# Two low halves and one copy of a graph network's flush put in another order, an earlier start of one product, and the first adjacency tile scaled by VectorE

## The chip, the cores and the metric

The kernel runs on one core of a Trainium2 chip. The metric is the time of one execution in microseconds (us) as the device reports it. Of the engines, TensorE is called PE, VectorE DVE, ScalarE ACT and GpSimd POOL in the profile; SP is the engine whose queue issues nearly all transfers (DMAs).

## What is computed

For each of 8 batches there are x (1024 rows of 512) and adj (1024 x 1024). Cut to what matters:

```python
# stage 0: four Gaussian kernels k over the entries of adj
w  = exp(-0.5 * (adj[..., None] - mu[k])**2 / (1e-14 + prec[k]**2))
ws = (w / w.sum(over k)).sum(over the row)            # one weight for each row and kernel
x1 = layernorm(x + concat_k(ws[k] * (x @ W[k].T)))
# stage 1: one of four experts for each batch
top1    = argmax(x1.mean(rows) @ router_w + router_b)
out     = adj @ (x1 @ expert_w[top1])
y       = batchnorm_by_expert(out) * gamma + beta     # sums over all batches of the expert
result  = layernorm(x1 + relu(y))
```

The batch norm needs sums over all batches, so the last stage (bn, relu, addition, layer norm) can start only when `out` is complete for the eighth batch.

## The kernel before, in words

**Tiles.** A batch is cut into T = 8 tiles of 128 rows, 64 tiles in all (TILES). Products of float32 values are made of three float16 products: each operand is cut into a high and a low half. `out` is kept turned, as (x1.T adj.T) through the expert: per batch there are eight z units (four 128-column pieces k of x1 by two halves of 512 rows; 24 matmuls of 128x512 each, into one of the two banks of `ps_z`) and eight o units (12 matmuls each, into the bank `ps_o`, which read the expert's planes `w_sel` and `zT`).

**Loop.** Every engine runs the same loop over n, and each has its work of step n written out by hand. Step n handles the weights of adj tile n, the x1 row block n - 1, the z unit n - 9 (`Z_LAG`) and the o unit n - 13 (`O_LAG`). After tile 63 the loop runs on to empty the pipe. In it `z_unit` and `o_units` say which units belong to which step. `FLUSH` is step 65: in step 64 PE makes z unit 55 (the seventh batch's last) and o unit 51, in step 65 o units 52 to 55 and z unit 56, in steps 66 to 68 z units 57 to 59, in step 69 z 60 and o 56, in step 70 o 57 and z 61, in step 71 o 58 and z 62, in step 72 o 59 and z 63, and after that o 60 to 63. `z_ahead_of_o` (line 289) says in which steps PE puts the z unit first.

**What a z unit waits for and who waits for it.** When PE has finished z unit u, ACT writes the high half (`take_z`, line 668 does the copy), and DVE the low half (`low_z`, line 884) from the same bank. z unit u + 2 needs that low half done, as it writes the same bank, and the first o unit of a half of a batch (`o_product`, k == 0) needs the low half of the fourth z unit of that half: o 52 waits for z 55, o 60 for z 63.

**What an o unit waits for.** ACT copies each o unit out of its bank (`take_o`, line 685) and DVE takes bn_stats of it (`o_stats`, line 904). There is one bank for o units, so o unit u waits until unit u - 1 is copied. From unit 53 on odd units use a second bank, half of `ps_t` (`second_bank`, line 267), which is free once the row sums of the last adj tile are done. The wait is line 1133 of the kernel: with `u > KEPT + 3` (KEPT is 50) only units from 54 on wait for the copy of u - 2 instead.

**DVE in a step** (lines 955 to 993): `y_stats` of x1 block n - 2, `low_z` of the z unit of step n - 1, `y_mean_var` of block n - 2, `o_stats` of the o units of step n - 1, `row_sums` of tile n - 1 (three products with accumulated sums, line 915), and then the additions to x1 (`weighted`, line 937) of block n - 1, mixed with the sums over kernels of tile n (line 953). When the o units of a batch are complete, `o_stats` aggregates four chunks (line 909). POOL cuts adj and x into halves (`cut_adj`, lines 500, 503, 505; `cut_x`) and, for each pair of blocks, normalises x1 and cuts it (`norm_pair`, lines 523 to 542); z units of a batch read these cuts.

**Start.** POOL scales adj tile 0 by 1024 in place (line 500, semaphore `pool_as`), then cuts it. ACT's first Gaussian (line 641) waits for that scaling and for two constants that POOL computes just ahead of it (`pool_gauss`), loads a register, and starts.

**Tail.** After o unit 63 DVE aggregates the last statistics, computes the batch norm's scales with ACT's help, and then the last stage runs over 64 row blocks: PE turns `out` back, DVE adds it to x1 (lines 1058, 1061) and takes statistics, ACT applies scales and squares, POOL normalises, SP stores. x1 and the outputs of the earlier batches were spilled to HBM and come back there. SP's queue is one sequence: the loads that need the space of `x1p` and `adjT` wait for z unit 63, the next ones for o unit 63, and the others and the stores for row blocks of the last stage.

Of the kernel before, what the change touches and what calls it, by code (L numbers as in the profile page):

```python
# [38 lines left out]
Z_LAG = 9  # L39
# [9 lines left out]
def gnn_program(nc, x, adj, mean_rel, prec_rel, w0, router_w, router_b, expert_w, gamma, beta, x1_spill,  # L49
# [15 lines left out]
    with ExitStack() as ctx:  # L65
# [3 lines left out]
        def sem(name):  # L69
            return ctx.enter_context(nc.semaphore(name))  # L70
# [76 lines left out]
        act_bn, act_affine, act_ssq, act_out = (sem(f"act_{k}") for k in ("bn", "affine", "ssq", "out"))  # L147
        pool_small, pool_out, pool_affine = (sem(f"pool_{k}") for k in ("small", "out", "affine"))
        act_lnv, act_std = sem("act_lnv"), sem("act_std")
        dve_nmr, dve_out, dve_affine = sem("dve_nmr"), sem("dve_out"), sem("dve_affine")  # L150

        dve_tot, dve_ws, dve_rest, dve_y, dve_stat, dve_mv = (
            sem(f"dve_{k}") for k in ("tot", "ws", "rest", "y", "stat", "mv"))
# [120 lines left out]
        def z_unit(n):  # L274

            if n <= Z_LAG + 2:
                return ((), (0,), (1, 2))[n - Z_LAG] if n >= Z_LAG else ()
            return range(n - Z_LAG, min(TILES, n - Z_LAG + 1))
# [9 lines left out]

        def z_ahead_of_o(n):

            return n == FLUSH - 1 or (n - O_LAG) % T == 0

        def ps_out(u):
            return ps_t[:, 0, :] if second_bank(u) else ps_o[:]
# [198 lines left out]
        def _(pool):  # L493
            g = nc.gpsimd

            def cut_adj(m):

                tile, cut = adj_in[:, m % ADJ_RING, :], adj_cut[:, m % 2]
                pool.wait_ge(adj_landed[m % ADJ_RING], 16 * (m // ADJ_RING + 1))
                g.tensor_scalar(tile, tile, ADJ_SCALE, 1.0, ALU.mult, ALU.mult).then_inc(pool_as, 1)  # L500
                pool.wait_ge(pool_as, m + 1)
                wait(pool, adj_turned[m % 2], 16 * (m // 2))
                g.tensor_scalar(cut[:, 0, :], tile, 1.0, 1.0, ALU.mult, ALU.mult).then_inc(pool_ah, 1)  # L503
                pool.wait_ge(pool_ah, m + 1)
                g.tensor_tensor(cut[:, 1, :], tile, cut[:, 0, :], ALU.subtract).then_inc(pool_al, 1)  # L505
# [125 lines left out]
        def _(act):  # L631
# [54 lines left out]

            for n in range(LAST):
                if n < TILES:
                    act.wait_ge(pool_as, n + 1)
                    wait(act, dve_ws, NK * (n - 1))  # L690
                    if n == 1:
                        act.wait_ge(pe_w0, C)
                    if n == 0:
                        act.wait_ge(pool_gauss, 2)
                    for j, k in enumerate(OTHERS):
                        if n == 0:
                            load_spread(k)
                        square(n, k, wgt[:, n % 2, j, :])
                if 1 <= n <= 2 * E:
                    e, part_ = expert_half(n - 1)  # L700
                    act.wait_ge(experts_landed[e], 16)
                    s.activation(planes(e)[:, 0, part_], expert_in(e)[:, part_], ACT.Copy, scale=W_SCALE).then_inc(act_whi, 1)
                if n - 1 == FLUSH - 1:
                    take_z(n - 1)
                take_o(n - 1)
                if n - 1 != FLUSH - 1:
                    take_z(n - 1)
                if 0 <= n - 1 < TILES:
                    sum_reciprocal(n - 1)
                if n < TILES:  # L710
                    weigh_others(n)
                    act.wait_ge(pool_al, n + 1)
                    if n == 0:
                        load_spread(SOLO)
                    square(n, SOLO, adj_in[:, n % ADJ_RING, :])
                    weigh_solo(n)
                if n == 0:
                    for c in range(C):
                        act.wait_ge(pe_w0, c + 1)
                        s.activation(w0T[:, 0, c, :], w0_banks[c], ACT.Copy, scale=W0_SCALE).then_inc(act_w0, 1)  # L720
# [76 lines left out]
        def _(dve):  # L797
# [3 lines left out]
            v.memset(ones_h[:], 1.0)  # L801
            v.memset(eps_bn, BN_EPS * (Z_SCALE * W_SCALE) ** 2)
            v.memset(eps_out, OUT_EPS)

            def split_w0():

# [91 lines left out]
            def o_stats(u):  # L898
                b, half, k = u // T, u % T // G, u % G
                if u == TILES - 1:  # L900
                    dve.wait_ge(pe_o, u + 1)
                else:
                    dve.wait_ge(act_o, u + 1)
                v.bn_stats(o_stat[:, b % 2, k, half, :], ps_out(u) if u == TILES - 1 else out_unit(u)).then_inc(dve_ostat, 1)
                if half == 1 and k == 3:
                    dve.wait_ge(dve_ostat, u + 1)
                    v.memset(pad, 0.0)
                    for c in range(C):
                        last = v.bn_aggr(o_mv[:, b, c, :], o_stat[:, b % 2, c, :, :].rearrange("p h s -> p (h s)"))
                    last.then_inc(dve_omv, 1)  # L910

            def row_sums(m):
                dve.wait_ge(act_rec, m + 1)
# [41 lines left out]
            for n in range(LAST):  # L955
                if 0 <= n - 2 < TILES:
                    y_stats(n - 2)
                for u in z_unit(n - 1):
                    low_z(u)
                if 0 <= n - 2 < TILES:  # L960
                    y_mean_var(n - 2)
                for u in o_units(n - 1):
# [11 lines left out]
                    v.tensor_tensor(sumT[:], sumT[:], ps_s[:, C:2 * C], ALU.add).then_inc(dve_sumT, 1)  # L974
                if 0 <= n - 1 < TILES:
                    row_sums(n - 1)
                else:
                    for k in range(5):
                        route(n, k)
# [97 lines left out]
        def _(pe):  # L1077
# [47 lines left out]
            def o_product(u):  # L1125
# [4 lines left out]
                    pe.wait_ge(dve_z, u + G)  # L1130
                if second_bank(u):
                    pe.wait_ge(dve_ws, NK * TILES)
                wait(pe, act_o, u - 1 if u > KEPT + 3 else u)
                for c in range(C):
                    for i, (left, right) in enumerate(PRODUCTS):
                        last = te.matmul(ps_out(u), w_sel[:, left, c, k * P:(k + 1) * P], zT[:, right, half, c, :],  # L1136
# [78 lines left out]
```

## Time and profile before

| | us |
|---|---|
| median of 3 runs | 892.62 |
| lowest and highest | 890.96, 893.26 |
| the profiled execution, its own time | 888.44 |
| span in the profile of that execution | 886.7 |

| engine | busy us | share of the span |
|---|---|---|
| PE matmul | 751.8 | 85% |
| DVE | 754.0 | 85% |
| ACT | 766.9 | 86% |
| POOL | 687.5 | 78% |

The span runs from the first instruction to the last landing, and the execution's own time is 1.7 us longer. A row of the timeline is: start and duration in us, engine, line of the kernel, operation, what it writes <- what it reads, shape, count, and in brackets how long the engine had been idle and for whom it waited. In the chain of waits (the chain that ended last, in order of time) a row is start, duration, engine, tile, line, and how many instructions are merged. A row of the windows view is a stretch of time, its length, the busy us (and instructions) of PE, PEld, DVE, ACT and POOL, the TensorE clock granted as a share of full speed, the mean busy share of the 16 DMA engines (it can come out slightly above 1) and GB/s.

### The profile page before, as it was taken

How to read it: one execution, taken by the hardware profiler on the slowest of the kernel's cores; microseconds unless marked ns; L12 is line 12 of the kernel's file. 1: busy time of each engine (PE TensorE's matmuls, PEld its weight loads, DVE VectorE, ACT ScalarE, POOL GpSimd, SP SyncE). 2: the span in 40 equal slices, each digit the busy share in tenths (PEclk: the TensorE clock that was granted, in tenths of full speed). 3: DMA queues.
4: the chain of work that ended last, by engine and by line, in shares of the span. 5: the costliest groups of instructions: out<-in, count | busy, mean ns of one | idle time of the engine just before them, and what ended most of it. 6: DMA issues, size and time to landing. Idle time of an engine off the chain costs nothing.

```text
span 886.7 us, 12501 instructions
## 1 busy us (share of the span) xinstructions
PE 751.8 (85%) x3922; PEld 349.1 (39%) x3922; DVE 754.0 (85%) x1639; ACT 766.9 (86%) x774; POOL 687.5 (78%) x773
## 2 busy tenths in 40 slices
PE   1444469899999999999999999999999989996671
PEld 1111124344444444444444444444444434444440
DVE  1999988899999999999999999999999981226994
ACT  5999998999999999999999999999999941116983
POOL 6699999999988888888888888888888441004794
PEclk9966679999999999999999999999999999998996
DMA  8799886898897779777977797789786636219999
GB/s 229 200 282 257 189 243 166 221 202 206 201 240 192 192 190 240 196 194 190 237 198 191 195 240 196 192 189 242 198 190 161 124 141 263 95 64 396 356 383 366
DMA packets 263925, 191.71 MB, mean 216 GB/s; under 512 B 210098, under 2 KB 210098, under 8 KB 262322
## 3 DMA queue, kind: packets, MB, share of 16 engines
q1 hardware_dynamic: 263714, 190.90, 79.3%
q8 instruction: 31, 0.51, 0.2%
q14 instruction: 36, 0.29, 0.1%
q10 hardware_dynamic: 144, 0.00, 0.0%
HBM read 91.78 MB, written 48.76 MB: 159 GB/s over the span
## 4 chain that ended last, share of the span: by engine, by line
ACT 38%; DVE 27%; POOL 19%; PE 9%; issue 4%; DMA 1%; SPq 0%; POOLq 0%; DVEq 0%; ACTq 0%
DVE ps_t L953 19%; ACT wgt L647 13%; ACT ps_t L656 6%; ACT ps_t L658 6%; ACT adj_in L641 5%; ACT ps_t L652 5%; PE ps_z L1118 5%; POOL adj_cut L505 3%; DVE x_in L937 3%; DVE wgt L915 3%; PE ps_o L1136 2%; POOL adj_in L500 2%; POOL x_turn L516 2%; PE ps_t L1136 2%; POOL adj_cut L503 2%
## 5 line engine op out<-in xcount | busy, mean ns | idle before, releaser
L1118 PE MATMUL ps_z<-adjT,x1p 128*128 128x512 f16 x1536 | 341.7, 379 | 0.5 <-POOL x1p L542 0.5
L953 DVE TENSOR_TENSOR ps_t<-ps_t,wgt 128x1024 f32<-128x1024 f32 x192 | 234.8, 1223 | 28.0 <-ACT ps_t L652 26.9
L1104 PE MATMUL ps_h<-w0T,x_turn 128*128 128x512 f16 x768 | 194.5, 407 | 75.1 <-DVE x_in L937 64.2
L915 DVE SCALAR_TENSOR_TENSOR wgt<-wgt,ps_t 128x1024 f32<-128x1024 f32 x192 | 224.7, 1214 | 15.8 <-ACT ps_t L658 15.8
L1118 PEld LDWEIGHTS ps_z<-adjT,x1p 128*128 128x128 f16 x1536 | 150.0, 98 | 181.3 <-POOL x1p L542 1.0
L641 ACT ACTIVATE wgt<-adj_in,neg_mu 128x1024 f32<-128x1024 f32 x192 | 205.6, 1134 | 8.4 <-POOL adj_in L500 8.2
L647 ACT ACTIVATE wgt<-wgt 128x3072 f32<-128x3072 f32 x64 | 176.5, 2758 | 0.0
L1136 PE MATMUL ps_o<-zT,w_sel 128*128 128x512 f16 x696 | 159.7, 379 | 4.8 <-DVE zT L884 3.5
L1104 PEld LDWEIGHTS ps_h<-w0T,x_turn 128*128 128x128 f16 x768 | 75.0, 103 | 184.4 <-issue 105.1
L505 POOL TENSOR_TENSOR adj_cut<-adj_in,adj_cut 128x1024 f16<-128x1024 f32 x64 | 136.6, 2134 | 5.4
L1136 PEld LDWEIGHTS ps_o<-zT,w_sel 128*128 128x128 f16 x696 | 67.9, 98 | 87.7 <-DVE zT L884 4.5
L937 DVE SCALAR_TENSOR_TENSOR x_in<-ps_h,wsum,x_in 128x128 f32<-128x128 f32 x256 | 82.4, 343 | 8.9 <-PE ps_h L1104 0.2
L884 DVE SCALAR_TENSOR_TENSOR zT<-ps_z,zT 128x512 f16<-128x512 f32 x64 | 43.1, 673 | 52.2 <-ACT zT L668 52.2
L542 POOL TENSOR_TENSOR x1p<-x_in,x1p 128x512 f16<-128x512 f32 x64 | 76.0, 1187 | 5.3
L516 POOL TENSOR_TENSOR x_turn<-x_in,x_turn 128x512 f16<-128x512 f32 x64 | 74.2, 1159 | 5.3
L500 POOL TENSOR_SCALAR adj_in<-adj_in 128x1024 f32<-128x1024 f32 x64 | 69.5, 1086 | 11.2 <-DMA adj_in<-in_adj_dram 5.9
L641 ACT ACTIVATE adj_in<-adj_in,neg_mu 128x1024 f32<-128x1024 f32 x64 | 72.8, 1138 | 0.0
L503 POOL TENSOR_SCALAR adj_cut<-adj_in 128x1024 f16<-128x1024 f32 x64 | 67.6, 1057 | 5.3
L668 ACT ACTIVATE zT<-ps_z 128x512 f16<-128x512 f32 x64 | 37.2, 582 | 39.3 <-PE ps_z L1118 39.3
L656 ACT ACTIVATE ps_t<-ps_t 128x1024 f32<-128x1024 f32 x64 | 64.6, 1009 | 5.9 <-DVE ps_t L953 3.8
L652 ACT ACTIVATE ps_t<-adj_in 128x1024 f32<-128x1024 f32 x64 | 65.8, 1028 | 3.0 <-DVE wgt L915 0.6
L658 ACT ACTIVATE ps_t<-ps_t 128x1024 f32<-128x1024 f32 x64 | 64.5, 1008 | 2.0
(220 smaller groups left out, 774.2 us busy)
## 6 DMA issues: line engine op xcount, KB each, us to landing
adj_in<-in_adj_dram SPq DMA_DIRECT2D x64, 512.0 KB, 4.1
x_in<-in_x_dram SPq DMA_DIRECT2D x64, 256.0 KB, 4.3
x_spill<-x_in SPq DMA_DIRECT2D x28, 512.0 KB, 3.4
out_spill<-o_stage SPq DMA_DIRECT2D x50, 256.0 KB, 3.1
w_sel<-w_planes SPq DMA_DIRECT2D x8, 1024.0 KB, 7.5
adjT<-x_spill SPq DMA_DIRECT2D x6, 1024.0 KB, 10.1
out_dram<-adjT SPq DMA_DIRECT2D x5, 1024.0 KB, 6.7
adjT<-out_spill SPq DMA_DIRECT2D x4, 1024.0 KB, 12.7
```

What stands on the lines that cost most here:

```text
L505: g.tensor_tensor(cut[:, 1, :], tile, cut[:, 0, :], ALU.subtract).then_inc(pool_al, 1)
L641: s.activation(to, adj_in[:, n % ADJ_RING, :], ACT.Square, bias=neg_mu[:, k:k + 1], scale=spread[k]).then_inc(act_sq, 1)
L647: s.activation(w, w, ACT.Exp, scale=-1.0).then_inc(act_w, 1)
L652: s.activation(tot, adj_in[:, n % ADJ_RING, :], ACT.Exp, scale=-1.0).then_inc(act_solo, 1)
L656: s.activation(tot, tot, ACT.Ln, scale=SUM_SCALE).then_inc(act_ln, 1)
L658: s.activation(tot, tot, ACT.Exp, scale=-1.0).then_inc(act_rec, 1)
L915: v.scalar_tensor_tensor(out=wgt[:, m % 2, j, :], in0=wgt[:, m % 2, j, :], scalar=SUM_SCALE / W0_SCALE, in1=tot, op0=ALU.mult, op1=ALU.mul ...
L937: last = v.scalar_tensor_tensor(out=row[:, f], in0=ps_h[:, m % 2, f], scalar=wsum[:, m % 2, COLUMN[k]:COLUMN[k] + 1], in1=row[:, f], op0=A ...
L953: v.tensor_tensor(tot, tot, wgt[:, n % 2, j, :], ALU.add).then_inc(dve_tot, 1)
L1104: last = te.matmul(ps_h[:, n % 2, :], xT[:, n % 2, left, c, :], w0T[:, right, c, :], start=(c + i == 0), stop=(c == C - 1 and i == 2))
L1118: last = te.matmul(ps_z[:, u % 2, :], x1p[:, b % 2, left, t, k * P:(k + 1) * P], adjT[:, b % 2, right, t, half * HALF:(half + 1) * HALF], ...
L1136: last = te.matmul(ps_out(u), w_sel[:, left, c, k * P:(k + 1) * P], zT[:, right, half, c, :], start=(c + i == 0), stop=(c == C - 1 and i = ...
```

## The change

1. **Start.** DVE instead of POOL scales adj tile 0, as soon as the tile has landed (`dve_as`). POOL's cut of the tile and ACT's first Gaussian wait for DVE. POOL's count `pool_as` is one lower for all later tiles.
2. **Seventh batch's last z.** In DVE's step 64 the low half of z unit 55 is made right behind `row_sums(63)`, ahead of the additions to x1 of block 63, and no longer in step 65 behind `y_stats(63)`.
3. **One more unit in the free bank.** o unit 53 waits for the copy of o unit 51 and no longer for that of 52.
4. **Last z.** In step 72 PE makes z unit 63 ahead of o unit 59, and ACT makes the high half of z 63 ahead of the copy of o 59.
5. **Statistics.** For the last batch the aggregation of chunk k follows its own bn_stats, so one aggregation instead of four stands behind the last o unit. Each of the four has a wait and a one-column memset of its own.

```diff
@@ -147,7 +147,7 @@
         act_bn, act_affine, act_ssq, act_out = (sem(f"act_{k}") for k in ("bn", "affine", "ssq", "out"))
         pool_small, pool_out, pool_affine = (sem(f"pool_{k}") for k in ("small", "out", "affine"))
         act_lnv, act_std = sem("act_lnv"), sem("act_std")
-        dve_nmr, dve_out, dve_affine = sem("dve_nmr"), sem("dve_out"), sem("dve_affine")
+        dve_nmr, dve_out, dve_affine, dve_as = sem("dve_nmr"), sem("dve_out"), sem("dve_affine"), sem("dve_as")
 
         dve_tot, dve_ws, dve_rest, dve_y, dve_stat, dve_mv = (
             sem(f"dve_{k}") for k in ("tot", "ws", "rest", "y", "stat", "mv"))
@@ -288,7 +288,11 @@
 
         def z_ahead_of_o(n):
 
-            return n == FLUSH - 1 or (n - O_LAG) % T == 0
+            return z_taken_first(n) or (n - O_LAG) % T == 0
+
+        def z_taken_first(n):
+
+            return n in (FLUSH - 1, TILES - 1 + Z_LAG)
 
         def ps_out(u):
             return ps_t[:, 0, :] if second_bank(u) else ps_o[:]
@@ -497,8 +501,11 @@
 
                 tile, cut = adj_in[:, m % ADJ_RING, :], adj_cut[:, m % 2]
                 pool.wait_ge(adj_landed[m % ADJ_RING], 16 * (m // ADJ_RING + 1))
-                g.tensor_scalar(tile, tile, ADJ_SCALE, 1.0, ALU.mult, ALU.mult).then_inc(pool_as, 1)
-                pool.wait_ge(pool_as, m + 1)
+                if m == 0:
+                    pool.wait_ge(dve_as, 1)
+                else:
+                    g.tensor_scalar(tile, tile, ADJ_SCALE, 1.0, ALU.mult, ALU.mult).then_inc(pool_as, 1)
+                    pool.wait_ge(pool_as, m)
                 wait(pool, adj_turned[m % 2], 16 * (m // 2))
                 g.tensor_scalar(cut[:, 0, :], tile, 1.0, 1.0, ALU.mult, ALU.mult).then_inc(pool_ah, 1)
                 pool.wait_ge(pool_ah, m + 1)
@@ -686,11 +693,12 @@
 
             for n in range(LAST):
                 if n < TILES:
-                    act.wait_ge(pool_as, n + 1)
+                    wait(act, pool_as, n)
                     wait(act, dve_ws, NK * (n - 1))
                     if n == 1:
                         act.wait_ge(pe_w0, C)
                     if n == 0:
+                        act.wait_ge(dve_as, 1)
                         act.wait_ge(pool_gauss, 2)
                     for j, k in enumerate(OTHERS):
                         if n == 0:
@@ -700,10 +708,10 @@
                     e, part_ = expert_half(n - 1)
                     act.wait_ge(experts_landed[e], 16)
                     s.activation(planes(e)[:, 0, part_], expert_in(e)[:, part_], ACT.Copy, scale=W_SCALE).then_inc(act_whi, 1)
-                if n - 1 == FLUSH - 1:
+                if z_taken_first(n - 1):
                     take_z(n - 1)
                 take_o(n - 1)
-                if n - 1 != FLUSH - 1:
+                if not z_taken_first(n - 1):
                     take_z(n - 1)
                 if 0 <= n - 1 < TILES:
                     sum_reciprocal(n - 1)
@@ -801,6 +809,8 @@
             v.memset(ones_h[:], 1.0)
             v.memset(eps_bn, BN_EPS * (Z_SCALE * W_SCALE) ** 2)
             v.memset(eps_out, OUT_EPS)
+            dve.wait_ge(adj_landed[0], 16)
+            v.tensor_scalar(adj_in[:, 0, :], adj_in[:, 0, :], ADJ_SCALE, None, ALU.mult).then_inc(dve_as, 1)
 
             def split_w0():
 
@@ -902,12 +912,16 @@
                 else:
                     dve.wait_ge(act_o, u + 1)
                 v.bn_stats(o_stat[:, b % 2, k, half, :], ps_out(u) if u == TILES - 1 else out_unit(u)).then_inc(dve_ostat, 1)
-                if half == 1 and k == 3:
+                chunks = range(C) if k == 3 else ()
+                if b == NB - 1:
+                    chunks = (k,)
+                if half == 1 and chunks:
                     dve.wait_ge(dve_ostat, u + 1)
                     v.memset(pad, 0.0)
-                    for c in range(C):
+                    for c in chunks:
                         last = v.bn_aggr(o_mv[:, b, c, :], o_stat[:, b % 2, c, :, :].rearrange("p h s -> p (h s)"))
-                    last.then_inc(dve_omv, 1)
+                    if k == 3:
+                        last.then_inc(dve_omv, 1)
 
             def row_sums(m):
                 dve.wait_ge(act_rec, m + 1)
@@ -955,8 +969,9 @@
             for n in range(LAST):
                 if 0 <= n - 2 < TILES:
                     y_stats(n - 2)
-                for u in z_unit(n - 1):
-                    low_z(u)
+                if n != FLUSH:
+                    for u in z_unit(n - 1):
+                        low_z(u)
                 if 0 <= n - 2 < TILES:
                     y_mean_var(n - 2)
                 for u in o_units(n - 1):
@@ -974,6 +989,9 @@
                     v.tensor_tensor(sumT[:], sumT[:], ps_s[:, C:2 * C], ALU.add).then_inc(dve_sumT, 1)
                 if 0 <= n - 1 < TILES:
                     row_sums(n - 1)
+                    if n == FLUSH - 1:
+                        for u in z_unit(n):
+                            low_z(u)
                 else:
                     for k in range(5):
                         route(n, k)
@@ -1130,7 +1148,7 @@
                     pe.wait_ge(dve_z, u + G)
                 if second_bank(u):
                     pe.wait_ge(dve_ws, NK * TILES)
-                wait(pe, act_o, u - 1 if u > KEPT + 3 else u)
+                wait(pe, act_o, u - 1 if u > KEPT + 2 else u)
                 for c in range(C):
                     for i, (left, right) in enumerate(PRODUCTS):
                         last = te.matmul(ps_out(u), w_sel[:, left, c, k * P:(k + 1) * P], zT[:, right, half, c, :],
```

## Rows read from the trace of the kernel before

**Rows 1.** Windows view: one stretch of the loop, one of the last stage

```profile
160.00:720.00 560.00, 546.26 (x2913) 248.69 (x2912) 529.53 (x1095) 550.35 (x507) 485.63 (x529) 1.00 0.80 198
...
812.00:876.00 64.00, 40.50 (x249) 27.80 (x247) 62.90 (x199) 54.78 (x115) 56.12 (x85) 0.93 1.03 379
```

**Rows 2.** ACT's waits, 20 to 721 us: total, times, longest

```profile
ACT ps_t L656 <- DVE ps_t L953: 3.8, 6, 1.0
```

**Rows 3.** The chain of waits, one o unit in the flush

```profile
784.80 2.59 PE ps_t L1136 x12
```

**Rows 4.** PE's waits, 700 to 887 us, for the low halves

```profile
PE ps_o L1136 <- DVE zT L884: 3.5, 2, 2.1
```

**Rows 5.** Timeline, the start

```profile
9.05 1.05 POOL L500 TENSOR_SCALAR adj_in<-adj_in 128x1024 f32<-128x1024 f32 x1
...
10.66 3.23 ACT L641 ACTIVATE wgt<-adj_in,neg_mu 128x1024 f32<-128x1024 f32 x3 [8.23 <-POOL adj_in L500]
...
25.84 1.20 DVE L967 SCALAR_TENSOR_TENSOR x1p<-adjT,x1p 128x1024 f16<-128x1024 f32 x1
...
25.92 2.03 POOL L500 TENSOR_SCALAR adj_in<-adj_in 128x1024 f32<-128x1024 f32 x1
```

**Rows 6.** Issue of adj tile 0 (timeline) and its time to landing (transfers view)

```profile
1.20 0.42 SPq L318 DMA_DIRECT2D adj_in<-in_adj_dram  x1
...
adj_in<-in_adj_dram SPq DMA_DIRECT2D x1, 512.0 KB, 6.8
```

**Rows 7.** Durations (ns, min/median/max) of two DVE lines that scale float32 in SBUF

```profile
L1027 DVE TENSOR_SCALAR wgt<-wgt,b_sb x4: 409/410/414, 808.8 to 809.7; 128x256 f32<-128x256 f32 x4
...
L1073 DVE TENSOR_SCALAR adjT<-adjT,adj_in x2: 535/726/916, 874.4 to 874.9; 128x512 f32<-128x512 f32 x2
```

**Rows 8.** Timeline, the flush of the seventh batch

```profile
725.18 1.13 DVE L937 SCALAR_TENSOR_TENSOR x_in<-ps_h,wsum,x_in 128x128 f32<-128x128 f32 x4
...
725.61 0.60 ACT L685 ACTIVATE adj_cut<-ps_o 128x512 f32<-128x512 f32 x1 [1.99 <-PE ps_o L1136]
...
726.95 0.67 DVE L884 SCALAR_TENSOR_TENSOR zT<-ps_z,zT 128x512 f16<-128x512 f32 x1
...
727.68 2.76 PE L1136 MATMUL ps_o<-zT,w_sel 128*128 128x512 f16 x12 [2.11 <-DVE zT L884]
...
730.48 0.60 ACT L685 ACTIVATE wgt<-ps_o 128x512 f32<-128x512 f32 x1 [4.27 <-PE ps_o L1136]
...
731.22 2.75 PE L1136 MATMUL ps_t<-zT,w_sel 128*128 128x512 f16 x12 [0.78 <-ACT wgt L685]
...
733.39 1.16 POOL L542 TENSOR_TENSOR x1p<-x_in,x1p 128x512 f16<-128x512 f32 x1
...
738.99 5.34 PE L1118 MATMUL ps_z<-adjT,x1p 128*128 128x512 f16 x24
```

**Rows 9.** Timeline, the last z unit and the last statistics

```profile
787.23 5.34 PE L1118 MATMUL ps_z<-adjT,x1p 128*128 128x512 f16 x24
...
792.60 0.36 SPq L414 DMA_DIRECT2D x1p<-x_spill  x1
...
793.24 0.69 DVE L884 SCALAR_TENSOR_TENSOR zT<-ps_z,zT 128x512 f16<-128x512 f32 x1 [6.41 <-ACT zT L668]
...
793.99 2.76 PE L1136 MATMUL ps_o<-zT,w_sel 128*128 128x512 f16 x12 [1.42 <-DVE zT L884]
...
805.42 0.30 DVE L909 BATCH_NORM_AGGREGATE o_mv<-o_stat 128x2 f32<-128x12 f32 x3
```

**Rows 10.** Windows view: transfers in the last stage

```profile
796.00:800.00 4.00, 4.00 (x20) 1.80 (x19) 0.69 (x1) 1.19 (x2) 0.00 (x0) 1.00 1.01 392
...
824.00:828.00 4.00, 2.88 (x19) 1.72 (x17) 4.00 (x15) 4.00 (x7) 1.85 (x4) 1.00 0.98 370
...
828.00:832.00 4.00, 2.79 (x18) 1.90 (x19) 4.00 (x13) 3.94 (x10) 1.41 (x2) 1.00 1.03 277
```

**Rows 11.** SP's last issue (timeline)

```profile
878.25 1.29 SPq L388 DMA_DIRECT2D out_dram<-adjT  x1
```

## What is predicted, and from what

> **What bounds the kernel now.** I read the windows view first, to see who is full in which stretch, then the waits of the engine that is full, and then the timeline of the few places that the change touches. In the 560 us of the loop ACT is busy for 550 and DVE for 530 [rows 1], and ACT's longest kind of wait on another engine over the whole loop comes to 3.8 us in 6 pieces [rows 2]. So the loop is a fixed cycle of ACT and DVE; nothing of the change is inside it, and what starts it earlier ends it earlier. After the last adj tile PE is the bound: the products of the flush stand in the chain one behind the other, an o unit at 2.59 us [rows 3] (a product that starts behind an idle PE shows 2.75; I take 0.16 as what two products in a row overlap), and a z unit at 5.34 - 0.16 = 5.18 us. PE waits only twice for a low half between the loop and the end, 3.5 us in all [rows 4]; those two are what parts 2 and 4 go for. The last stage is DVE without a break (62.9 of 64 us), beside DMA engines that are full as well (1.03) [rows 1]. Both start from the same two events, z unit 63 and o unit 63, and all they wait for comes after these, so I treat the last stage as one block that moves with its start.
>
> **Part 1, the start.** POOL's scaling ran from 9.05 to 10.10, and ACT's first Gaussian started at 10.66, that is 0.56 later, for the load of its register [rows 5]. The tile had been there since about 1.20 + 6.8 = 8.0 us [rows 6]; POOL only got to it at 9.05, because it had the two constants to make first. DVE does nothing at that time. What a scaling of 128x1024 float32 costs DVE no row shows; the nearest are 0.41 us for 256 columns and, at the least, 0.535 for 512 [rows 7]. That is 0.49 ns a column on a fixed 0.285, which gives 0.79 us for 1024, as an estimate from these rows. The upper end is the slow one of the two at 512 columns, 0.92, plus 512 columns at 0.92 / 512 = 1.8 ns, or 1.8 us. So DVE is done between 8.8 and 9.8. ACT also needs POOL's constants, which are there by 9.05 less a few hundredths. Its first Gaussian then starts at about 9.0 + 0.56 = 9.6 at best, and at 9.8 + 0.56 = 10.4 at worst: a gain of 0.3 to 1.1. I take 0.9, near the clean rows, as the tile lands while POOL does only operations on four columns. POOL gains about as much for its cuts (10.10 against some 9.2). What is next late is no DMA that I can find: POOL's scaling of tile 2 at 25.92 stood in its own queue behind x. DVE's new wait stands at the head of its queue and nothing of DVE is needed before ACT's first Gaussians are done.
>
> A row shows what a collision costs here: POOL's scaling at 25.92 took 2.03 us instead of 1.05, and DVE had begun a two-input operation at 25.84 that ended at 27.04; 27.04 + 1.05 - 0.1 is where POOL's ended [rows 5]. The Trainium skill's page "SBUF — State Buffer", section "Who interferes with whom", says the same of such pairs, and it says it too of a float32 tensor_scalar of VectorE in SBUF, which may take the port pair that it shares with GpSimd. By that rule this change brings a collision that was not there: DVE's scaling would hold up POOL's last constants from 8.0 to 8.8 and ACT's start would come out near 9.9, a gain of 0.8 instead of 0.9; no run shows that yet.
>
> **Part 2, z 55 low half.** DVE finished row_sums(63) just ahead of 725.18, did four additions and y_stats, and only then, at 726.95, the low half, for which PE waited 2.11 us until 727.68 [rows 8]. In the new place it starts at about 725.1 and ends at 725.8. Then o 52 has another wait that ends last: the copy of o 51 out of the only bank, 725.61 + 0.60 = 726.21 on ACT. From the end of an ACT copy to PE's start it takes 731.22 - 731.08 = 0.14 [rows 8]. So o 52 starts at 726.35, 1.33 earlier, and not 1.9. What is queued behind the moved half on DVE: four additions, y_stats and the aggregation of block 63, and POOL's last norm_pair behind these. The additions come 0.6 later, but the half no longer stands between y_stats and the aggregation, so the aggregation moves by 0 to 0.1. POOL ends its last cut at 733.39 + 1.16 = 734.55; z 56, which reads it, starts at 738.99 [rows 8] and will start near 736.7. Cover of 2.1 us left; a delay of POOL costs only beyond that.
>
> **Part 3, one more unit in the free bank.** o 53 started at 731.22 while its predecessor began at 727.68; back to back it would be 2.60. So 3.54 - 2.60 = 0.94 goes. Its bank is free: the row sums were done by 725.18. o 54 now needs the copy of o 52, which ends at about 726.35 + 2.80 + 0.60 = 729.8, before 731.5. Nothing takes the place of the wait. Parts 2 and 3 bring z 56 and all behind it 2.27 us forward; the routing, the load of the expert's planes and the units up to z 62 are launched by PE's own results and go with it.
>
> **Part 4, the last z.** o 60 started at 793.99 behind 1.42 us of idle time that ended with DVE's low half at 793.24 [rows 9]. With z 63 ahead of o 59, the copy (0.60) and the low half (0.69) lie beside 2.59 us of o 59: 0.2 + 0.60 + 0.69 + 0.1 = 1.6 us, so 1.0 of cover is left. z 63 has to find the low half of z 61 done, and that one is a whole z unit and an o unit back. o 59 goes in the second bank and o 60 needs the copy of o 58, both long free. The gain is 1.42 plus the overlap of 0.16, 1.58 us at o 60. At the end of z 63 it is 2.59.
>
> **Part 5, statistics.** Three aggregations took 0.30 us behind the last one [rows 9]; 0.25 to 0.30 of that goes from the path. The three others, each with a wait and a memset, go into DVE's idle time between o units.
>
> **Sum.** Start 0.9, flush 2.27, last z 1.58, statistics 0.27: o 63 and the batch norm come 0.9 + 2.27 + 1.58 + 0.27 = 5.0 us earlier. The end of z 63, at which the first loads of the last stage start (792.60) [rows 9], comes 0.9 + 2.27 + 2.59 = 5.8 earlier. Which of the two sets the end? The DMA engines are full from 796 on (1.01) and the span (886.7) ends 8.4 us behind the last store's issue at 878.25, while all engines of the last stage are done, so the end is a queue of transfers [rows 10, 11]. If it never ran empty, the end would move by 5.8. But the row of 824 to 828 shows 0.98, where the rows around it lie above 1 [rows 10]: there the queue had just run dry, waiting for stores that the last stage releases. A queue that ran dry forgets its head start. So I take 5.0. Of the profiled execution's 888.44 that makes 883.4 (span 881.7). The median of the runs shown is 4.2 above the profiled one; the difference is all that I forecast, so 892.6 - 5.0 = 887.6.
>
> **Rivals.**
> 1. *The start does not reach the end, or hardly.* The 0.9 (or 0.3) is swallowed where a load or the first products are later than ACT. For it: POOL and SP at the start are closely packed. Against it: ACT's small waits [rows 2]. Then 4.1 us: 888.5. 15%.
> 2. *The head start of the transfers is kept.* For it: 1.01 and more in nearly all rows of the last stage. Against it: the 0.98. Then 5.8 us: 886.8. 15%.
> 3. *The transfers give some back.* From 828 to 832 the engines are full at 277 GB/s instead of some 390 [rows 10]. That costs (390 - 277) / 390 x 4 = 1.2 us, and it is bound to how loads and stores meet. Loads of z 63 that come 0.8 further ahead of the rest meet other stores. If such a stretch appears twice more, the gain is 5.0 - 2.4 = 2.6 us: 890.0. 10%.
> 4. *Slower: the loop falls into another step.* The collision at 25.92 shows that POOL and DVE hold each other up depending on who comes first, by 1.0 us [rows 5]. POOL's start moves by another amount than ACT's, and if the loop then locks in a phase in which DVE is held up once in each of 64 tiles, the gain is gone at 5.0 / 64 = 0.08 us a tile; at 0.15 us a tile the time is 892.6 - 5.0 + 9.6 = 897.2. Against it: 560 us of loop leave ACT only 10 idle, and the phase is set by ACT and DVE themselves, which move together. 4%.
> 5. *The edits do not do what they say* (o 52 held by another wait, say): the flush gives half, 1.1 instead of 2.27, and 3.8 us in all: 888.8. 8%.
>
> **How the numbers follow.** The forecast as it stands, 5.0 give or take 0.6, has what is left, 48%. What a measurement of this kernel can tell from no change is about 0.3%, or 2.7 us; the three runs of before lie 2.3 apart. Faster by more than 2.7: the forecast, rivals 1, 2 and 5, and half of rival 3, less 7% because two medians of such runs may differ by more than a microsecond: 84%. Within 0.3%: 12%. Slower: 4%. The range takes in the bounds of part 1 (0.3 to 1.1), rival 2 above and rival 3 below, and some of the runs' own spread: gains of 2.2 to 7.0 us, 885.6 to 890.4.
>
> **What the profile of the changed kernel would show.** ACT's first Gaussian at 9.6 to 9.9 and a DVE scaling of 0.8 us that starts at 8.0. If ACT then keeps its step, row_sums(63) end near 724.1. Between the copy of o 51 and o 52 only 0.14 us, no wait of o 53, and z 56 starting 3.2 us earlier (735.8). No wait for a low half ahead of o 60, and o 60 at 789.2. One aggregation instead of four behind the last bn_stats. DVE's first addition of the last stage and SP's last store 5.0 earlier. I am wrong in the start if ACT's lead is smaller at 721 us than at 10; in the flush if DVE's half begins after 725.3 less the lead; in the last stage if DVE moves by 5.0 and the span by something else, which would mean that the transfers have a bound of their own.

## The result, and the profile after

The changed kernel has a median of 883.81 us in 5 runs (882.91 to 887.86), the kernel before one of 891.43 in 5. The ratio is 0.9932, with a 95% interval of 0.9915 to 0.9950: 6.1 us faster, between 4.5 and 7.6. (The ratio is not the quotient of the two medians, which lie 7.6 us apart; gains in us are worked out from the ratio throughout.) The forecast ratio, 887.6 / 892.6 = 0.9944, is inside that interval; the forecast time, 887.6, is 3.8 us above the median, and the median lies below the range, which began at 885.6. The direction was right; the forecast gain was too small, and the time that it was taken from was too high.

The profiled execution says something else at first sight. Its own time is 887.86 and its span 886.1, only 0.6 us under the 886.7 of the profiled execution before. To find the gain, the three parts of the span have to be read apart. First the start, in the timeline of the changed kernel:

```profile
7.30 1.41 POOL L563 TENSOR_TENSOR root<-two_var,minus_half 128x4 f32<-128x4 f32 x1
7.99 0.69 DVE L813 TENSOR_SCALAR adj_in<-adj_in 128x1024 f32<-128x1024 f32 x1 [6.98 <-DMA adj_in<-in_adj_dram]
8.32 0.41 POOL L564 TENSOR_SCALAR neg_mu<-neg_mu 128x4 f32<-128x4 f32 x1
8.97 0.20 POOL L567 TENSOR_TENSOR neg_mu<-neg_mu,root 128x4 f32<-128x4 f32 x1
9.80 3.23 ACT L648 ACTIVATE wgt<-adj_in,neg_mu 128x1024 f32<-128x1024 f32 x3 [7.37 <-POOL neg_mu L567]
```

DVE scales the tile in 0.69 us as soon as it has landed, and ACT starts its first Gaussian (the row of line 648) at 9.80 instead of 10.66 [rows 5]. ACT now waits for POOL's constants.

Then the loop. These are ACT's Exp of tiles 13, 14 and 63 (the last), before and after:

```profile
164.41 1.03 ACT L652 ACTIVATE ps_t<-adj_in 128x1024 f32<-128x1024 f32 x1
176.44 1.03 ACT L652 ACTIVATE ps_t<-adj_in 128x1024 f32<-128x1024 f32 x1
...
713.89 1.03 ACT L652 ACTIVATE ps_t<-adj_in 128x1024 f32<-128x1024 f32 x1
```

```profile
163.79 1.03 ACT L659 ACTIVATE ps_t<-adj_in 128x1024 f32<-128x1024 f32 x1
180.07 1.03 ACT L659 ACTIVATE ps_t<-adj_in 128x1024 f32<-128x1024 f32 x1
...
717.21 1.03 ACT L659 ACTIVATE ps_t<-adj_in 128x1024 f32<-128x1024 f32 x1
```

The step from tile 13 to 14 took 12.03 us before and 16.28 after. Up to there the changed kernel leads by 0.62, behind it it is 3.63 late, and 3.32 at the end of the loop. No edit touches this place. PE was waiting there for the first expert's planes, for 4.08 us where it had waited 1.33 before, and then ran at a lower clock (timeline of PE before, timeline of PE after, windows view after):

```profile
157.60 2.75 PE L1104 MATMUL ps_h<-w0T,x_turn 128*128 128x512 f16 x12 [2.35 <-DVE x_in L937]
...
166.86 2.76 PE L1136 MATMUL ps_o<-zT,w_sel 128*128 128x512 f16 x12 [1.33 <-DMA w_sel<-w_planes]
```

```profile
159.57 5.34 PE L1136 MATMUL ps_z<-adjT,x1p 128*128 128x512 f16 x24
168.99 4.25 PE L1154 MATMUL ps_o<-zT,w_sel 128*128 128x512 f16 x12 [4.08 <-DMA w_sel<-w_planes]
173.03 3.00 PE L1122 MATMUL ps_h<-w0T,x_turn 128*128 128x512 f16 x12
```

```profile
170.00:172.00 2.00, 2.00 (x7) 0.73 (x5) 0.00 (x0) 0.00 (x0) 1.83 (x3) 0.53 1.10 272
```

An o unit takes 2.75 us at the full granted clock and 4.25 here. The granted clock between 170 and 172 is 0.53, which is the lower of TensorE's two levels, 1.2 instead of 2.4 GHz, after 4.08 us without a matmul.

Last, the flush and the end, in the timeline of the changed kernel:

```profile
729.66 2.75 PE L1154 MATMUL ps_o<-zT,w_sel 128*128 128x512 f16 x12 [0.78 <-ACT adj_cut L692]
...
732.25 2.75 PE L1154 MATMUL ps_t<-zT,w_sel 128*128 128x512 f16 x12
...
740.02 5.34 PE L1136 MATMUL ps_z<-adjT,x1p 128*128 128x512 f16 x24
...
780.49 10.52 PE L1136 MATMUL ps_z<-adjT,x1p 128*128 128x512 f16 x48
...
791.04 0.36 SPq L418 DMA_DIRECT2D x1p<-x_spill  x1
791.68 0.69 DVE L894 SCALAR_TENSOR_TENSOR zT<-ps_z,zT 128x512 f16<-128x512 f32 x1 [3.82 <-ACT zT L675]
793.44 2.75 PE L1154 MATMUL ps_o<-zT,w_sel 128*128 128x512 f16 x12
...
877.63 1.31 SPq L392 DMA_DIRECT2D out_dram<-adjT  x1
```

Taken from the last Exp of the loop (713.89 before, 717.21 after), the lines that answer to rows 8, 9 and 11 stand so (the statistics' end is the start and duration of the last aggregation, 804.74 + 0.20 in the changed kernel):

| from the last Exp to | before | after | gain | forecast |
|---|---|---|---|---|
| o unit 52 | 13.79 | 12.45 | 1.34 | 1.33 |
| z unit 56 | 25.10 | 22.81 | 2.29 | 2.27 |
| first load of the last stage | 78.71 | 73.83 | 4.88 | 4.86 |
| o unit 60 | 80.10 | 76.23 | 3.87 | 3.85 |
| end of the last aggregation | 91.83 | 87.73 | 4.10 | 4.12 |
| SP's last issue | 164.36 | 160.42 | 3.94 | 4.12 |
| end of the span | 172.81 | 168.89 | 3.92 | 4.12 |

So behind the loop everything came within 0.2 us of what had been worked out. What made the profiled execution long lies in the loop. The other four executions took 882.9 to 884.6, so they can hardly have lost as much there; no profile shows them.

### The profile page after: what moved, and what is told of

The parts are those of the page before. It is cut to its first block, busy times and chain, and to the rows that moved or that the text cites. A ratio compares the mean times of both kernels' runs of the same rounds, so it can differ in the third digit from the quotient of the medians.

```text
span 886.1 us, 12505 instructions
## 1 busy us (share of the span) xinstructions
PE 753.0 (85%) x3922; PEld 349.8 (39%) x3922; DVE 755.4 (85%) x1643; ACT 766.9 (87%) x774; POOL 687.7 (78%) x772
## 4 chain that ended last, share of the span: by engine, by line
ACT 35%; DVE 26%; POOL 19%; PE 12%; issue 4%; DMA 2%; SPq 0%; POOLq 0%; DVEq 0%; ACTq 0%
DVE ps_t L967 19%; ACT wgt L654 12%; PE ps_z L1136 6%; ACT ps_t L663 6%; ACT ps_t L665 5%; ACT adj_in L648 5%; ACT ps_t L659 5%; POOL adj_cut L512 3%; DVE x_in L951 3%; PE ps_o L1154 3%; DVE wgt L929 3%; POOL x_turn L523 2%; POOL adj_in L507 2%; PE ps_t L1154 2%; POOL adj_cut L510 2%
```

## The experiments

Theory A: the parts add up as their idle times say, 5.0 us in all. Theory B: the start also decides how the loop meets its transfers. The first four kernels take the change apart.

**Start alone** (`e1_start`).

```diff
+            dve.wait_ge(adj_landed[0], 16)
+            v.tensor_scalar(adj_in[:, 0, :], adj_in[:, 0, :], ADJ_SCALE, None, ALU.mult).then_inc(dve_as, 1)
...
+                if m == 0:
+                    pool.wait_ge(dve_as, 1)
```

> Only part 1 (DVE scales adj tile 0). Theory A, the parts add up as read from the profile: 0.6 to 0.9 us faster than the kernel before. Theory B, the start also decides in which phase the loop meets the transfers, and the load of the first expert's planes (at 160 us) is then late by less: the medians differ by 0.9 plus some 2.5, so 3 to 4 us faster, although no edit touches the loop. In the profile: PE's wait for w_sel at o unit 0, 1.3 us in the profile of before and 4.1 in that of the changed kernel, and the start of the tile-by-tile Exp of ACT at tiles 13 and 14.

Measured: 889.48 (12 runs) against 890.77 (30 runs), ratio 0.9979 [0.9963, 0.9994], 1.9 us. By the ratio that lies between the two theories: A's 0.9 is inside the interval, and B's 3 us are at its edge.

**Flush alone** (`e2_flush`).

```diff
-                for u in z_unit(n - 1):
-                    low_z(u)
+                if n != FLUSH:
+                    for u in z_unit(n - 1):
+                        low_z(u)
...
-                wait(pe, act_o, u - 1 if u > KEPT + 3 else u)
+                wait(pe, act_o, u - 1 if u > KEPT + 2 else u)
```

> Only parts 2 and 3 (low half of z unit 55 ahead of x1's additions, o unit 53 no longer behind the copy of 52). Theory A: 2.3 us faster (1.33 and 0.94). Theory B says the same of this edit, as the loop is not moved. In the profile PE's wait of 2.11 us ahead of o 52 becomes 0.78 and that of 0.78 ahead of o 53 is gone.

Measured: 888.13 (12 runs), ratio 0.9966 [0.9948, 0.9984], 3.0 us, between 1.4 and 4.6, which holds A's 2.3 as well; PE's wait ahead of o 52 is 0.78 in its profile, and none stands ahead of o 53.

**Last z alone** (`e3_lastz`).

```diff
-            return n == FLUSH - 1 or (n - O_LAG) % T == 0
+            return n in (FLUSH - 1, TILES - 1 + Z_LAG) or (n - O_LAG) % T == 0
```

> Only part 4 (z unit 63 ahead of o unit 59 on PE and ACT). Both theories: the wait of 1.42 us ahead of o 60 is gone and the kernel is 1.6 us faster; if the first loads of the last stage keep their head start it is 2.6 us.

Measured: 889.94 (12 runs), ratio 0.9985 [0.9969, 1.0], 1.3 us, where 1.6 was expected. The wait ahead of o 60 is gone. But its profiled execution took 892.9, and that is where a mechanism missing from the prediction came to light. This is PE in the flush, where this kernel is the same as before, and the windows view of it:

```profile
731.02 4.45 PE L1140 MATMUL ps_o<-zT,w_sel 128*128 128x512 f16 x12 [2.12 <-DVE zT L888]
736.25 2.75 PE L1140 MATMUL ps_t<-zT,w_sel 128*128 128x512 f16 x12 [0.78 <-ACT wgt L689]
```

```profile
730.00:735.00 5.00, 3.98 (x11) 1.53 (x12) 1.65 (x5) 0.00 (x0) 3.42 (x6) 0.66 1.05 403
```

It is the same wait as in rows 8 (2.11 us there), but o 52 took 4.45 us instead of 2.76, because the granted clock behind that idle time was the lower one (0.66 on average over the 5 us). The wait of 2.1 us can cost 3.8.

**All but the start** (`e4_all_but_start`, parts 2 to 5).

> Parts 2 to 5 without part 1. Theory A: 2.27 + 1.58 + 0.27 = 4.1 us faster, 0.6 to 0.9 short of the whole change. Theory B: 4.1 us faster as well, but that is about 3.5 us short of the whole change, whose median was 7.6 us under that of before.

Measured: 886.46 (7 runs), ratio 0.9944 [0.9923, 0.9965], 5.0 us. With the 1.9 of the start alone this makes 6.9, with the parts' own 3.0 and 1.3 and the statistics (0.3) it makes 6.5; the whole was 6.1. So the parts add up within their intervals, which are 1.4 to 1.9 us wide to each side. Theory B's large part of the start is not seen.

Next, which executions are typical? And does the first load of the planes, which PE awaits at o unit 0, set the scatter?

**The kernel before, once more** (`e5_before_again`, no edit), **and the changed kernel, once more** (`e6_after_again`).

> The kernel before, unchanged, under a new name, for a second profile of it. Theory C, the profiled execution of before was a lucky one: in it the load of the first expert's planes was issued at 160.49, behind an issue of x that took 0.39 us, while in the five other profiles that issue took 1.25 to 1.59 and o unit 0 came later. Then this profile shows tile 14 of ACT's Exp 13.5 to 16 us behind tile 13 (12.03 in the first profile) and an execution near 890 to 892. Rival: the first profile is typical and the loss is made elsewhere, so tile 14 again takes 12.0. The times: the same as before within 0.2%.

> The changed kernel, unchanged, on the same chip as the kernel before. Fixed sum: 5.0 us faster (0.9944), an execution of the profile near 883 to 886. If the parts are worth more than their idle times (the single parts came out at 1.9, 3.0 and 1.3 us, all but start at 5.0), 6 to 7 us faster (0.992 to 0.9935).

Measured: 890.49 (12 runs) against 891.26 (23 runs) for the kernel before, ratio 0.9997 [0.9976, 1.0018], and 885.76 (6 runs) for the changed one, ratio 0.993 [0.9903, 0.9956], 6.2 us. The second profile of before took 891.6. Its tile 14 came 12.64 behind tile 13, less than theory C wanted, and in its flush stands the lower clock (timeline and windows view of the kernel before, second profile; and the windows view of the first):

```profile
728.74 4.45 PE L1136 MATMUL ps_o<-zT,w_sel 128*128 128x512 f16 x12 [2.12 <-DVE zT L884]
```

```profile
728.00:734.00 6.00, 4.48 (x13) 1.57 (x14) 1.37 (x5) 0.60 (x1) 4.62 (x8) 0.72 1.04 403
```

```profile
727.00:733.00 6.00, 4.54 (x21) 1.95 (x22) 1.30 (x5) 0.60 (x1) 4.68 (x8) 1.00 1.04 403
```

One kernel, two executions: after the same idle time the clock was 0.72 on average over the 6 us in one and 1.00 in the other. The span of the second profile is 3.1 us longer than that of the first; 1.7 of it are here, 1.1 were lost by the end of the loop. The 1.7 reach the end of the kernel: SP's last issue came 164.36 us behind the last Exp of the loop in the first profile and 166.11 in the second.

**The planes first** (`e7_before_planes_first` on the kernel before, `e8_after_planes_first` on the changed one).

```diff
-                if n + 2 < TILES:
-                    load_adj(n + 2)
-                if n + 3 < TILES:
-                    load_x(n + 3)
+                early = u % T == 0 and 0 <= u < TILES - T
+                if not early:
+                    load_adj and load_x as above
...
                     sp.dma_start(w_sel[:], w_planes[e]).then_inc(w_landed, 16)
+                if early:
+                    load_adj and load_x as above
```

> The kernel before, with one order changed in SP's queue: at the start of a batch's o units (first seven batches) the load of the expert's planes is issued ahead of the loads of adj and x instead of behind them. Theory C: the wait of PE for w_sel ahead of o unit 0 (1.1 to 4.1 us in six profiles) goes, tile 14 takes 11 to 11.5 us, the median is 2 to 4 us lower and the scatter of the times smaller. Rival, the level is made elsewhere: less than 1 us. Risk: adj and x land later and POOL waits.

> The changed kernel with the same order in SP's queue. Theory C: 2 to 4 us less than the changed kernel on the same chip, 8 to 10 under the kernel before, and PE's wait for w_sel gone. Rival: as the changed kernel.

Measured: on the kernel before 891.67 (12 runs), ratio 1.0 [0.9982, 1.0019], and a scatter as wide as ever (889.1 to 894.5): theory C, which wanted 2 to 4 us less, falls. On the changed kernel 884.04 (6 runs), ratio 0.9922 [0.9895, 0.9949], against 885.76 for the changed kernel on the same chip; the intervals overlap. But on the kernel before the edit did less than was meant: in its profile the load of the planes was issued at 160.66, no earlier than the 160.49 of the first profile of before, as the transfers ahead of it stood 0.7 us later, and PE still waited 1.25 us for it. Tile 14 came 11.95 behind tile 13, the shortest step of all profiles, but at tiles 18 and 19 the loop lost 2.5 us (PE's timeline and the windows view, kernel before with the planes first):

```profile
213.60 0.82 PE L1125 MATMUL ps_z<-adjT,x1p 128*128 128x512 f16 x3 [1.37 <-POOL x1p L549]
...
215.07 4.37 PE L1111 MATMUL ps_h<-w0T,x_turn 128*128 128x512 f16 x12
```

```profile
215.00:220.00 5.00, 5.00 (x25) 1.99 (x22) 4.33 (x9) 4.97 (x5) 4.67 (x5) 0.66 0.43 134
```

The 12 products at 215.07 took 4.37 us instead of 2.75 at a granted clock of 0.66, here after a stretch with a wait of 1.4 us and with 32 matmuls of one column. The same stood ahead of tile 14 in the changed kernel with the planes first. No wait for the planes was left, but the products of x in front of them were slow behind their wait:

```profile
157.00 4.44 PE L1129 MATMUL ps_h<-w0T,x_turn 128*128 128x512 f16 x12 [2.35 <-DVE x_in L958]
```

That wait of 2.35 us is in every one of the 14 profiles of this document (in the first profile of before it stands at 157.60, with 2.75 behind it), and it tells where the step to tile 14 gets its scatter. From the start of these products to the z unit behind them it took 2.6 us in six profiles, at a clock of 1.00, and 3.9 to 4.3 in eight (0.50 to 0.70 over the first 3 us). The step to tile 14 is the time from that start to o unit 0, 9.19 to 12.66 us, and 2.75 to 2.77 more, in 13 profiles. In the 14th, that of the changed kernel, it is 1.50 more again, just what o unit 0 lost there at the lower clock (4.25 instead of 2.75). So a part of this scatter is the clock, and the rest is when the planes land.

**Is it the clock?** The last four kernels ask this. `e9_wait53` is the line of part 3 alone, `e10_low55` the first half of the diff of the flush alone (with its counterpart behind `row_sums`). `e11_before_kept_busy` is the kernel before with idle time filled:

```diff
+                if n == FLUSH:
+                    pe.wait_ge(dve_y, TILES - 1)
+                    for _ in range(9):
+                        te.matmul(ps_h[:, 0, :], w_sel[:, 0, 0, 0:P], zT[:, 0, 0, 0, :], start=True, stop=True)
                 for u in o_units(n):
                     o_product(u)
```

> Only part 3 (o unit 53 not behind the copy of 52). The idle time of 2.11 us ahead of o 52 stays. Idle times alone: 0.94 us faster. If the rest of what the flush edits brought beyond their idle times is TensorE's clock, which in three of five profiles with that idle time stood at 0.96 between 700 and 745 us and in all five without it at 1.00, this edit alone must not bring it: 0.9 us, no more.

> Only part 2 (low half of z unit 55 ahead of x1's additions). Idle times alone: 1.33 us faster. With the clock: 1.33 and the drop that goes with it; o unit 52 took 4.45 us instead of 2.75 at the lower clock in one profile, 1.7 more, in three of five profiles, which makes 1.0 on average: 2.3 us faster, and the granted clock between 700 and 745 us at 1.00.

> The kernel before with 9 matmuls more, whose results nobody reads, in PE's idle time ahead of o unit 52; they read w_sel and zT and write the free half of ps_h. No wait is shortened. Clock theory: granted clock 1.00 between 700 and 745 us in each profile, o 52 takes 2.75 us, and the median is about 1.0 us lower (it falls by 1.7 where it would have dropped). Rival, the clock has nothing to do with the idle time: the same as before, or 0.1 slower.

Measured, against 890.97 (29 runs): wait53 889.64 (12 runs), ratio 0.9999 [0.9983, 1.0016]; low55 888.95 (12), 0.9988 [0.9974, 1.0002]; kept busy 889.77 (12), 0.9983 [0.9967, 1.0]. In the last kernel no wait of the chain is shorter (o 52 starts 13.80 us behind the last Exp, as before), 9 matmuls are added, and it is 1.5 us faster by the ratio, with an interval that ends at no change. Its PE and its clock where the wait was:

```profile
729.05 2.11 PE L1162 MATMUL ps_h<-zT,w_sel 128*128 128x512 f16 x9
731.34 2.76 PE L1136 MATMUL ps_o<-zT,w_sel 128*128 128x512 f16 x12 [0.18 <-DVE zT L884]
```

```profile
730.00:736.00 6.00, 5.04 (x24) 1.96 (x23) 1.96 (x5) 0.60 (x1) 4.10 (x7) 1.00 1.03 396
```

Its profiled execution, 892.3, is the slowest of its 12 all the same: the step to tile 14 took 15.43 us in it.

Over all profiles the count is this. With the idle time of 2.1 us ahead of o 52 the clock between 700 and 745 us was 0.96 in four (`e3`, `e5`, `e7`, `e9`) and 1.00 in two (the first profile of before, `e1`). Without it, whether by the edit or by the filling, it was 1.00 in all eight. Four of six against none of eight shows that the idle time brings the lower clock; the kernel kept busy adds one profile to the eight, and two of the six kept the clock without filling. What the lower clock costs on average is not resolved by the timed runs. The two single edits make 0.1 and 1.1 us by the ratio where 0.9 and 2.3 were expected (1.3 and 2.0 by the medians), with an interval of 1.5 and 1.2 us to both sides; the second is closer to its idle time alone, 1.33, than to 2.3. The profiles split the flush plainly. z unit 56 starts 25.10 us behind the last Exp in the kernel before and 23.75 with part 2 alone, 1.35 less; with part 3 alone it starts at 25.85, 0.95 less than the 26.80 of the kernel before in the profile with the lower clock; with both it is 22.81. The kernel with part 3 alone kept the lower clock in its profile (o 52 took 4.21 us), as expected.

**The planes first and the even units in the second bank** (`e12_planes_first_even_bank`, on the changed kernel).

```diff
-            return u > KEPT + 2 and u % 2 == 1
+            return u > KEPT + 1 and u % 2 == 0
...
-                wait(pe, act_o, u - 1 if u > KEPT + 2 else u)
+                wait(pe, act_o, u - 1 if u > KEPT + 1 else u)
```

> The changed kernel with the expert's planes loaded ahead of adj and x, and with the even units from o 52 on in the second bank instead of the odd ones from 53 on, so that o 52 need not wait for the copy of o 51. PE's wait of 0.78 us ahead of o 52 becomes 0.2 to 0.3; 0.5 us under the changed kernel with the planes first, 7 to 8 us under the kernel before.

Measured: 883.40 (6 runs), ratio 0.9919 [0.99, 0.9937], 7.2 us under the kernel before, the fastest of all; its advantage over the changed kernel (6.1 and 6.2) is within the intervals. The 0.5 us expected from the second bank do not show: with the planes first alone it was 7.0. In PE's timeline o 52 no longer waits for a copy:

```profile
722.23 2.75 PE L1161 MATMUL ps_o<-zT,w_sel 128*128 128x512 f16 x12
725.11 2.76 PE L1161 MATMUL ps_t<-zT,w_sel 128*128 128x512 f16 x12
```

Counted from the last Exp, SP's last issue comes 0.67 us earlier than with the planes first alone, but the end of the span does not (169.00 against 168.19).

## Why the prediction was right and wrong

**Part 1.** Forecast 0.9, measured 0.86 at ACT's first Gaussian. At the end of the loop it was worth a little more. In all five profiles with the early start the step to tile 36 took 10.99 (10.98 to 10.99), in all nine others it took 11.33 to 11.35; why, no run shows. In four of the five 0.3 to 0.4 was given back at tile 3 (in `e1_start` nothing), which two profiles without the early start show as well. If the steps to tiles 12 and 14 are left out, the start brings some 1.1 us. The start alone measured 1.9 [0.5, 3.3]. The term was mis-sized by 0.2. In the profile of the changed kernel my own sign of being wrong came true: ACT led by 0.86 at 10 us and was 3.3 late at the end of the loop. The step to tile 14 had swallowed the lead. The cost of DVE's scaling came from two distant rows as 0.79; it was 0.69. What the Trainium skill's page "SBUF — State Buffer" ("Who interferes with whom") says of such a scaling, that it can contend with GpSimd, was seen: beside it POOL's two operations on four columns took 1.41 and 0.41 us instead of 1.03 and 0.20. The first of them had begun at 7.30, ahead of DVE's 7.99, and was stretched all the same. POOL's last constant started at 8.97 instead of 8.77, and ACT waited for it. I had put the gain at 0.8 with that rule and at 0.9 without; the first Gaussian started at 9.66 to 9.80 in the five profiles with the early start and at 10.60 to 10.66 in the others, so both figures fit.

**Parts 2 to 5 in the profile.** Every gain from the last Exp on was right within 0.2 us (table above): the copy of o 51 became the wait that ends last ahead of o 52, z 56 found POOL ready, and nothing replaced the wait of o 60.

**Which event sets the end.** I took the 4.1 us of o 63 and not the 4.9 of the first loads, since a queue that has run dry forgets its head start. Counted from the last Exp, the end moved by 3.92. A single profile could not tell 4.1 from 4.9, but several can: in the four with parts 2 to 5 and the old bank (`e4`, `e6`, `e8` and the changed kernel) the end lies 168.2 to 169.2 us behind the last Exp, 168.8 on average, and in the three with none of them and the clock at 1.00 (before, `e1`, `e11`) 172.8 to 173.1, 173.0 on average, which is 4.2. The row of after that answers to rows 10 fits a head start that is lost there, a share of 0.81 where 0.98 stood:

```profile
824.00:828.00 4.00, 2.75 (x18) 1.68 (x16) 4.00 (x14) 4.00 (x8) 1.09 (x3) 1.00 0.81 280
```

Rival 2 would by its size fit the measured time (5.8 against 6.1), but the ends just counted speak against it, and SP's last issue moved by 3.9 only. Rival 3 did not come. Rival 1 did not, as the lead of the start is still there behind the loop in each profile if the step to tile 14 is taken out. Rival 4 (the loop in another step) did not: the loop's ordinary steps are 10.95 to 10.99 in all kernels. Rival 5 is excluded by the table.

**The step that failed** is the last of the sum, with the price of PE's waits that it takes over: "The median of the runs shown is 4.2 above the profiled one; the difference is all that I forecast, so 892.6 - 5.0". Two things are wrong in it.

First, the level. The 892.62 was the median of three executions of a kernel that scatters between 888.3 and 896.8 in later runs, and the later medians are 890.5 to 891.4. That makes the forecast 1.2 us too high, counted from the 891.43 of the result. The 4.2 us between it and the profiled execution, which I named and passed over, was the sign: in the profiled execution the lower clock came neither at o 52 nor at the products of x ahead of tile 14, and the planes of the first expert cost 1.33 us of waiting where it was up to 4.08 in others. The range should have taken in that spread to both sides; I widened it only by some of it. How far the miss depends on the sample shows in `e6_after_again`: there the changed kernel had a median of 885.76, which lies just inside the range from 885.6.

Second, the size. A wait of PE was priced at its idle time. Its price is the idle time and, in four of six profiles, another 1.7 us (4.45 - 2.75) for the products after it: 4 / 6 x 1.7 = 1.1 us on average. With it the flush is worth 2.27 + 1.1 = 3.4 (measured alone: 3.0), and the sum becomes 1.1 + 3.4 + 1.58 + 0.27 = 6.3 us (measured: 6.1 and 6.2). From 891.3, about what the kernel before has in the later runs, this gives 885.0, between the two medians measured, 883.8 and 885.8. This sum was made after the fact. The profiles show the lower clock, its 1.7 us and that they reach the last store. How often it comes is known from six profiles only, and the intervals of the result (4.5 to 7.6), of the flush alone (1.4 to 4.6) and of all but the start (3.1 to 6.9) each hold the sum with this term and the sum without it.

**What stays open.** Why the planes of the first expert are issued and land at such different times was not found, nor what decides whether the clock falls behind one and the same wait. The step to tile 14 lay between 12.0 and 16.3 us over the kernels that have the old order of loads; in the three of them with the early start it was 14.4, 14.5 and 16.3, in the eight others 12.0 to 15.4, and whether the early start makes it longer was not tested; loading the planes first shortened that step to 11.95, 12.21 and 12.21 in three profiles without moving the median of the kernel before. Why that median did not move was not found either. How the gain splits between parts 2 and 3 is settled in the profiles and not in the timed runs.

## What to carry to other kernels

Compare a profiled execution with the other runs before a sum is made on it: if it lies 4 us under their median, something in it went unusually well, and its rows under-price what a removed wait usually costs. Price an idle time of TensorE as the idle time and a chance of the lower clock behind it, and count that chance at its own place, over several profiles. And where a stage has transfers that fill the DMA engines, look for the place where their queue runs dry; in this kernel the end moved with the event behind that place.

## What the runs showed of the hardware

The granted clock fell after idle times of TensorE as short as 2.1 us (o 52: 4.45 us instead of 2.75), in some executions of a kernel and not in others: behind the 2.1 us ahead of o 52 in four of six profiles, behind the 2.35 us ahead of the products of x at 157 us in eight of 14, and behind the six waits of 1.9 to 3.2 us ahead of o unit 0 in none. The Trainium skill's page "TensorE: Matmul & The Clock Gate", section "Part 1: The HAM clock gate (the "warmup" mystery)", says that the gate's watch runs free of the kernel, so that the same kernel can come out differently; the two profiles of the kernel before, 1.00 and 0.72 over 6 us around o 52, agree. With nine matmuls in the idle time, whose results nobody reads, the clock stayed at 1.00 in the one profile taken. And a DVE scaling of float32 in SBUF ran 1024 columns in 0.69 us, and stretched POOL's operations of four columns beside it by 0.2 to 0.4 us.
